# Weight fold and FFN on one core: x transposed in strips 1 to 3 of the fold only, four transpositions at a time

## The chip, the cores and the metric

One core of a Trainium2 chip runs the program. The metric is the device time of one execution in microseconds. TensorE is PE in the profile (PEld its weight loads), VectorE is DVE, ScalarE is ACT, the queue of SyncE that issues every DMA is SP.

## What is computed

```python
# x (8, 512, 2048), itok (8,), weight (2048, 2048), lora_a (8, 16, 2048), lora_b (8, 2048, 16), codes (2048, 2048)
base = jnp.einsum('bsi,oi->bso', x, weight) + bias
low = jnp.einsum('bsi,bri->bsr', x, a_sel)          # a_sel = lora_a[adapter_id]
delta = jnp.einsum('bsr,bor->bso', low, b_sel)
y = base + scale[:, None, None] * delta
w = _dequant_nf4(codes, absmax)
out = x + jnp.einsum('bsd,od->bso', y, w) + bias2
```

All in float32. The kernel multiplies the two weight matrices first (the "fold"), and then x by the folded matrix.

## The kernel before

**Two stages.** The fold makes W = w times weight, in NS = 4 strips of 512 output columns. A strip is 17 jobs (`S1`), 68 in all (`JOBS`); job g is step s = g mod 17 of strip g // 17. In a job PE multiplies one tile of `weight` (in step 0 the columns of lora_b) with the strip's dequantised codes `wq`: 16 k-steps of three matmuls 128x512 (`three`, lines 1035 to 1037; float32 is split into a high and a low half, and the third small product is left out). In the first step of a strip 32 bias matmuls follow (lines 1115 and 1116). The second stage then multiplies x by the folded matrix in 448 products, by a scheme with seven products in place of eight (A11, A12, S2, SS1, S3, S4, A22), whose operands are sums of blocks.

**What else the fold does, job by job.** All engines go through the jobs in one fixed order that is written out by hand.
- DVE: in odd steps from 3 on, and in step 0, the sums of the folded weights (`weight_sums`, 797 to 802), one dequantisation of a 128x512 piece of codes for the next strip in strips 0 to 2 (`dequantise_a` and `_b`, 741 to 773), sums of x (`x_sum`, 808 to 818), the low halves of the next job's tile (`split_lo`, 788, two) and of a transposed piece (`piece_lo`, 782).
- ACT: copies the last job's result out of PSUM (`evacuate`, 563), then the factors for the piece (`make_downs`, 538 and 540), the high halves of the next tile (`split_hi`, 553), the ladders and rungs of the next piece (`make_ladders` 517 and 518, `make_ups` 526 to 533), the high half of a transposed piece (`piece_hi`, 547), and the copies of transposed x (`copy_group`, 571).
- PE: beside the matmuls, four transpositions of a dequantised piece together (`transpose_piece`, 1030, after k-step 9 or 4), and those of x.
- SP: the DMAs, in one queue. It waits in its program order, and what stands behind a waiting DMA waits too. The second half of the tile for job g + 2 is loaded when job g is done; the first half when half of job g is done.

**x in the fold.** x is brought into the scheme's form here: 128 groups of 128x512. A group is loaded into `x_nat` (three buffers), transposed by four PE instructions into `tr_x` (two PSUM banks), copied by ACT into `rq`, which has one 2 KB slot for each of the seven blocks. Four groups are a unit (32 units); DVE makes four sums of a unit, and one DMA of 1792 KB stores all seven blocks to `xc_d` (`store_x_sums`, line 311). The first copy of the next unit waits for that store. `groups_of` places the groups: one in an odd job, three in an even one, in jobs 1 to 64; a transposition stands alone between two k-steps:

```python
for c, i in enumerate(groups):
    if 0 <= k - x_start[c] < QK:
        transpose_x(i, k - x_start[c])
```

The sums of weights go by a DMA of 896 KB (`store_w_sums`, line 316) every second job. In strips 0 and 2 the two stores fall in the same job, in strips 1 and 3 in different ones.

## Time and profile before

| | |
|---|---|
| median of 3 runs | 2314.99 us (2314.47 to 2316.05) |
| the profiled execution, its own time | 2315.77 us |
| its span | 2314.0 us |
| PE busy | 2210.7 us (96%) |
| DVE busy | 1684.9 us (73%) |
| ACT busy | 1115.7 us (48%) |
| DMA, mean | 238 GB/s, 75.8% of 16 engines' span |
| jobs of the fold end between | 161 and 983.5 us |
| four x transpositions, PE, x512 | 271 ns each |

The page gives busy time by engine and by line; a busy PE there is an upper measure, since the spans of pipelined matmuls overlap. Where the fold ends a job, ACT copies the result at once, so the start of line 563 on ACT is the job's end on PE to within 0.05 us. The difference of two such starts is a job's length.

### The profile page before, as it was taken

How to read it: one execution, taken by the hardware profiler on the slowest of the kernel's cores; microseconds unless marked ns; L12 is line 12 of the kernel's file. 1: busy time of each engine (PE TensorE's matmuls, PEld its weight loads, DVE VectorE, ACT ScalarE, POOL GpSimd, SP SyncE). 2: the span in 40 equal slices, each digit the busy share in tenths (PEclk: the TensorE clock that was granted, in tenths of full speed). 3: DMA queues.
4: the chain of work that ended last, by engine and by line, in shares of the span. 5: the costliest groups of instructions: out<-in, count | busy, mean ns of one | idle time of the engine just before them, and what ended most of it. 6: DMA issues, size and time to landing. Idle time of an engine off the chain costs nothing.

```text
span 2314.0 us, 37569 instructions
## 1 busy us (share of the span) xinstructions
PE 2210.7 (96%) x15112; PEld 2012.9 (87%) x15112; DVE 1684.9 (73%) x2400; ACT 1115.7 (48%) x1494; POOL 0.2 (0%) x4
## 2 busy tenths in 40 slices
PE   1389999999999999999999999999999999999999
PEld 1368877887888787899999999999999999999999
DVE  8888886897888434387777776666776666776665
ACT  6666665675666333254444443333444433433332
POOL 0000000000000000000000000000000000000000
PEclk9799999999999999999999999999999999999999
DMA  5248885888687699777777887777887787877775
GB/s 119 69 151 260 256 269 187 267 261 254 221 267 244 207 301 290 248 249 242 236 231 240 262 258 242 241 245 242 277 267 240 241 246 243 297 246 240 240 244 173
DMA packets 399331, 550.51 MB, mean 238 GB/s; under 512 B 41624, under 2 KB 256280, under 8 KB 399032
## 3 DMA queue, kind: packets, MB, share of 16 engines
q1 hardware_dynamic: 399160, 548.12, 75.8%
q8 instruction: 121, 1.98, 0.3%
q14 instruction: 50, 0.41, 0.1%
HBM read 421.66 MB, written 127.42 MB: 237 GB/s over the span
## 4 chain that ended last, share of the span: by engine, by line
PE 56%; DMA 0%; DVE 0%; issue 0%; ACT 0%; DVEq 0%
PE ps L1037 18%; PE ps L1035 18%; PE ps L1036 18%; PE ps L1078 1%; DMA comb_raw<-wc_d 0%; PE ps L1067 0%; ACT comb L584 0%; DVE res L903 0%; DVE res L910 0%; DVE res L888 0%; DVE low_st L848 0%; DVE comb L825 0%; DVEq L908 0%
## 5 line engine op out<-in xcount | busy, mean ns | idle before, releaser
L1035 PE MATMUL ps<-comb,xs 128*128 128x256 f32 (+1 forms) x3584 | 1014.6, 283 | 0.9 <-issue 0.9
L1037 PE MATMUL ps<-comb,xs 128*128 128x256 f32 (+1 forms) x3584 | 1014.7, 283 | 0.0
L1036 PE MATMUL ps<-comb,xs 128*128 128x256 f32 (+1 forms) x3584 | 1009.3, 282 | 0.0
L589 ACT CAST xs<-xr 128x1024 fp32r<-128x1024 f32 x427 | 447.8, 1051 | 638.9 <-DMA xr<-xc_d 638.2
L831 DVE TENSOR_TENSOR xs<-xr,xs 128x1024 fp32r<-128x1024 f32 x427 | 522.5, 1224 | 299.7 <-ACT xs L589 297.4
L1036 PEld LDWEIGHTS ps<-comb,xs 128*128 128x128 f32 x3584 | 677.8, 189 | 5.3
L1035 PEld LDWEIGHTS ps<-comb,xs 128*128 128x128 f32 x3584 | 676.7, 189 | 1.3 <-issue 1.3
L1037 PEld LDWEIGHTS ps<-comb,xs 128*128 128x128 f32 x3584 | 676.7, 189 | 0.0
L1035 PE MATMUL ps<-wq,tile 128*128 128x512 f32 x1088 | 477.4, 439 | 3.4 <-DVE wq L782 3.4
L1037 PE MATMUL ps<-wq,tile 128*128 128x512 f32 x1088 | 428.9, 394 | 0.0
L1036 PE MATMUL ps<-wq,tile 128*128 128x512 f32 x1088 | 427.2, 393 | 0.0
L1035 PEld LDWEIGHTS ps<-wq,tile 128*128 128x128 f32 x1088 | 206.2, 189 | 73.0 <-DVE wq L782 3.8
L1037 PEld LDWEIGHTS ps<-wq,tile 128*128 128x128 f32 x1088 | 205.7, 189 | 45.6
L1036 PEld LDWEIGHTS ps<-wq,tile 128*128 128x128 f32 x1088 | 207.9, 191 | 22.5 <-issue 1.0
L788 DVE TENSOR_TENSOR tile<-raw,tile 128x1024 fp32r<-128x1024 f32 x136 | 161.6, 1220 | 35.2 <-ACT tile L553 35.2
L553 ACT CAST tile<-raw 128x1024 fp32r<-128x1024 f32 x136 | 138.9, 1048 | 48.6 <-DMA raw<-in_L_cond_weight_dram 45.5
L1046 PE MATMUL ps<-ident,x_nat 128*128 128x128 f32 x512 | 139.0, 271 | 0.0
L1030 PE MATMUL ps<-ident,wq_nat 128*128 128x128 f32 x256 | 44.2, 301 | 86.8 <-DVE wq_nat L773 86.8
L1030 PEld LDWEIGHTS ps<-ident,wq_nat 128*128 128x128 f32 x256 | 34.0, 154 | 98.7 <-DVE wq_nat L773 79.5
L563 ACT COPY cs<-ps 128x512 f32<-128x512 f32 x64 | 37.6, 588 | 161.2 <-PE ps L1037 161.2
L571 ACT COPY rq<-ps 128x512 f32<-128x512 f32 x128 | 75.2, 587 | 55.7 <-PE ps L1046 42.6
L910 DVE TENSOR_TENSOR res<-ps,res 128x512 f32<-128x512 f32 x128 | 88.6, 692 | 14.0 <-DVE res L880 0.5
(92 smaller groups left out, 1710.1 us busy)
## 6 DMA issues: line engine op xcount, KB each, us to landing
xr<-xc_d SPq DMA_DIRECT2D x427, 512.0 KB, 4.0
raw<-in_L_cond_weight_dram SPq DMA_DIRECT2D x128, 512.0 KB, 4.5
xc_d<-rq SPq DMA_DIRECT2D x32, 1792.0 KB, 7.5
x_nat<-in_x_dram SPq DMA_DIRECT2D x128, 256.0 KB, 3.8
res<-in_x_dram SPq DMA_DIRECT2D x64, 512.0 KB, 5.5
out_dram<-res SPq DMA_DIRECT2D x128, 256.0 KB, 5.0
wc_d<-cs SPq DMA_DIRECT2D x32, 896.0 KB, 4.6
comb_raw<-wc_d SPq DMA_DIRECT2D x28, 1024.0 KB, 8.3
```

The lines of the kernel that those rows point to most:

```text
L553: nc.scalar.copy(tile[slot][:, HI, :, :], raw[slot][:, LO, :, :]).then_inc(s_hi, 1)
L563: nc.scalar.copy(cs[:, h:h + 5:4, :], acc[g % 2][:, :].rearrange("p (c o) -> p c o", c=2)).then_inc(s_evac, 1)
L571: nc.scalar.copy(rq[:, GROUP_OF[r], :, :], tr_x[i % 2][:, :].rearrange("p (t s) -> p t s", t=QK)).then_inc(s_xcp, 1)
L589: nc.scalar.copy(xs[f][:, HI, :, :], xr[f][:, LO, :, :]).then_inc(s_xhi, 1)
L788: tt(tile[slot][:, LO, :, :], raw[slot][:, LO, :, :], tile[slot][:, HI, :, :].bitcast(F32), ALU.subtract).then_inc(s_lo, 1)
L831: tt(xs[f][:, LO, :, :], xr[f][:, LO, :, :], xs[f][:, HI, :, :].bitcast(F32), ALU.subtract).then_inc(s_xlo, 1)
L910: tt(dst, bank_d[u][:, :], dst, ALU.add).then_inc(s_lev, 1)
L1030: last = nc.tensor.transpose(tr_q[n % 2][:, t * P:(t + 1) * P], wq_nat[n % 2][:, t * P:(t + 1) * P], ident[:, :])
L1035: nc.tensor.matmul(out_ap, t_hi, m_hi, start=first, stop=False)
L1036: nc.tensor.matmul(out_ap, t_hi, m_lo, start=False, stop=False)
L1037: return nc.tensor.matmul(out_ap, t_lo, m_hi, start=False, stop=last)
L1046: ins = nc.tensor.transpose(tr_x[i % 2][:, t * P:(t + 1) * P], x_nat[i % 3][:, t * P:(t + 1) * P], ident[:, :])
```

## The change

- `x_step(i)` puts group i after k-step 3 + 6i counted from the first k-step of job 17. So 128 groups take 48 jobs (17 to 64), and none stands in strip 0. Three jobs (a round, 48 k-steps) hold eight groups, two units: the first job after k-steps 3, 9 and 15, the second after 5 and 11, the third after 1, 7 and 13.
- The four transpositions of a group follow each other.
- `x_nat` has two buffers instead of three; SP loads group i + 2 when group i is transposed. The freed 2 KB hold `a21_t`: the first group of a unit is copied there, not into the slot of S3, so that it need not wait for a store.
- A unit's blocks go to memory by two DMAs: A11 and A12 (512 KB, `store_x_blocks`) once ACT has copied them, the other five (1280 KB, `store_x_sums`) when the sums are made. The second copy of the next unit waits for the store of the five, the third for that of the two.
- The copies, sums, loads and stores are placed by `groups_in` in bands of k-steps. A copy whose transposition stands after k-step 8 to 10 comes behind the ladders on ACT, one after k-step 0 to 3 ahead of `split_hi`, one after 11 or later at the next job's head.

```diff
-    GROUP_OF = [S3, A22, A11, A12]
+    GROUP_OF = [None, A22, A11, A12]
...
+    def x_step(i):
+        return S1 * KT + 6 * i + 3
+
+    def groups_in(g, first, last):
+        return [i for i in range(4 * UNITS) if KT * g + first <= x_step(i) < KT * g + last]
...
-        x_nat = [at(f"x_nat{i}", 176 + 2 * i, [P, QD], F32) for i in range(3)]
+        x_nat = [at(f"x_nat{i}", 176 + 2 * i, [P, QD], F32) for i in range(2)]
+        a21_t = at("a21_t", 180, [P, QK, P], F32)
...
-                if i >= 3:
-                    sp.wait_ge(s_tr, i - 2)
+                if i >= 2:
+                    sp.wait_ge(s_tr, i - 1)
...
                 sp.wait_ge(s_sums, 4 * (m + 1))
-                sp.dma_start(xc_d[p, :, :, c * QK:(c + 1) * QK, :].rearrange("f p k t -> p f k t"),
-                             rq[:, :, :, :]).then_inc(s_xst, 16)
+                sp.dma_start(xc_d[p, S2:, :, c * QK:(c + 1) * QK, :].rearrange("f p k t -> p f k t"),
+                             rq[:, S2:, :, :]).then_inc(s_xst, 16)
+
+            def store_x_blocks(m):
+                p, c = divmod(m, 2)
+                sp.wait_ge(s_xcp, 4 * (m + 1))
+                sp.dma_start(xc_d[p, :S2, :, c * QK:(c + 1) * QK, :].rearrange("f p k t -> p f k t"),
+                             rq[:, :S2, :, :]).then_inc(s_xsa, 16)
...
-                if g % 2 == 0 and len(ahead) > 2:
-                    load_group(ahead[2])
+                n = pieces_of(g)
+                for k in range(KT):
+                    for i in groups_in(g, k - 1, k):
+                        if i + 2 < 4 * UNITS:
+                            load_group(i + 2)
+                    if k == 8 and g + 2 < JOBS:
+                        load_half(g + 2, 0)
+                    for i in groups_in(g, k - 4, k - 3):
+                        if i % 4 == 3:
+                            store_x_blocks(i // 4)
+                    for i in groups_in(g, k - 8, k - 7):
+                        if i % 4 == 3:
+                            store_x_sums(i // 4)
+                    if k == 11 and n is not None and n + 2 < NS * PIECES:
+                        load_codes(n + 2)
...
                 act.wait_ge(s_tr, i + 1)
                 if r == 0 and m:
+                    act.wait_ge(s_sums, 4 * m - 2)
+                if r == 1 and m:
                     act.wait_ge(s_xst, 16 * m)
-                nc.scalar.copy(rq[:, GROUP_OF[r], :, :], tr_x[i % 2][:, :].rearrange("p (t s) -> p t s", t=QK)
+                if r == 2 and m:
+                    act.wait_ge(s_xsa, 16 * m)
+                nc.scalar.copy(rq[:, GROUP_OF[r], :, :] if r else a21_t[:, :, :], tr_x[i % 2][:, :].rearrange("p (t s) -> p t s", t=QK)
...
+                for i in groups_in(g, 8, 11):
+                    copy_group(i)
                 for i in turned_in(g):
                     piece_hi(i)
...
+            def transpose_x(i):
+                pe.wait_ge(s_xn[i % 2], 16 * (i // 2 + 1))
...
+                for t in range(QK):
+                    last = nc.tensor.transpose(tr_x[i % 2][:, t * P:(t + 1) * P], x_nat[i % 2][:, t * P:(t + 1) * P],
+                                               ident[:, :])
```

**SP's queue around job 41** (strip 2, step 7; `wc_d` is the weight sums' store, `xc_d` the x store, `raw` half a tile, `code_t` codes). Before, job 41:

```order
L316 DMA wc_d<-cs 128x7x256
L311 DMA xc_d<-rq 128x7x512
L298 DMA raw_57<-in_L_cond_weight_dram 128x8x128
L282 DMA code_t<-in_L_ffn_codes_dram 128x512
L306 DMA x_nat_69<-in_x_dram 128x512
L298 DMA raw_58<-in_L_cond_weight_dram 128x8x128
```

Now job 41, a first job of a round:

```order
L325 DMA wc_d<-cs 128x7x256
L320 DMA xc_d<-rq 128x2x512
L309 DMA x_nat_67<-in_x_dram 128x512
L314 DMA xc_d<-rq 128x5x512
L301 DMA raw_57<-in_L_cond_weight_dram 128x8x128
L309 DMA x_nat_68<-in_x_dram 128x512
L285 DMA code_t<-in_L_ffn_codes_dram 128x512
L301 DMA raw_58<-in_L_cond_weight_dram 128x8x128
```

Now the end of job 42 and the beginning of job 43, the round's third job:

```order
L314 DMA xc_d<-rq 128x5x512
L301 DMA raw_56<-in_L_cond_weight_dram 128x8x128
L325 DMA wc_d<-cs 128x7x256
L309 DMA x_nat_68<-in_x_dram 128x512
L309 DMA x_nat_67<-in_x_dram 128x512
```

The x store is in two parts with a load of x between them, and in the third job a load of x stands behind the stores and half a tile.

**ACT in job 41.** Before, from the evacuation to the last rung:

```order
L563 COPY cs<-ps 128x2x256
L571 COPY rq<-ps 128x512
L538 ACTIVATE rung_a<-ladder_61 128x512
L540 ACTIVATE rung_b<-ladder_61 128x512
L553 CAST tile_51<-raw_55 128x1024
L553 CAST tile_52<-raw_56 128x1024
L517 ACTIVATE ladder_60<-code_t,consts 128x512
L518 ACTIVATE ladder_60<-code_t,consts 128x512
L547 CAST wq_50<-ps 128x4x128
L526 ACTIVATE wq_nat_62<-ladder_60,consts 128x512
```

Now, from the second half of the tile on:

```order
L564 CAST tile_52<-raw_56 128x1024
L528 ACTIVATE ladder_60<-code_t,consts 128x512
L529 ACTIVATE ladder_60<-code_t,consts 128x512
L586 COPY rq<-ps 128x512
L558 CAST wq_50<-ps 128x4x128
L537 ACTIVATE wq_nat_62<-ladder_60,consts 128x512
```

The copy of a unit's second group (line 586 here) stands inside the job, ahead of the piece's cast and of the rungs for the next piece; before, the copy that waited for the store stood at the next job's head.

## Rows read from the trace of the kernel before

**Rows 1.** Windows; job pairs of strips 2 and 3, one store.
```profile
core 0: us, PE busy (x) PEld busy (x) DVE busy (x) ACT busy (x) POOL busy (x), PEclk, DMA share, GB/s
603.20:627.88 24.68, 24.68 (x122) 19.85 (x121) 22.00 (x34) 16.96 (x26) 0.00 (x0) 1.00 0.84 262
635.00:638.00 3.00, 3.00 (x17) 2.38 (x16) 2.90 (x5) 3.00 (x6) 0.00 (x0) 1.00 1.02 362
807.40:831.20 23.80, 23.80 (x113) 19.04 (x112) 9.01 (x12) 7.32 (x10) 0.00 (x0) 1.00 0.97 304
```

**Rows 2.** Timeline of ACT, one row at a job's end: strips 2, 3, last jobs.
```profile
603.25 0.59 ACT L563 COPY cs<-ps 128x512 f32<-128x512 f32 x1 [1.59 <-PE ps L1037]
...
627.93 0.59 ACT L563 COPY cs<-ps 128x512 f32<-128x512 f32 x1 [1.59 <-PE ps L1037]
...
819.47 0.59 ACT L563 COPY cs<-ps 128x512 f32<-128x512 f32 x1 [6.35 <-PE ps L1037]
...
843.28 0.59 ACT L563 COPY cs<-ps 128x512 f32<-128x512 f32 x1 [4.51 <-PE ps L1037]
...
972.68 0.59 ACT L563 COPY cs<-ps 128x512 f32<-128x512 f32 x1 [6.00 <-PE ps L1037]
...
983.56 0.59 ACT L563 COPY cs<-ps 128x512 f32<-128x512 f32 x1 [8.16 <-PE ps L1037]
```

**Rows 3.** Timeline of ACT and PE where strip 1 begins.
```profile
333.86 0.59 ACT L563 COPY cs<-ps 128x512 f32<-128x512 f32 x1 [1.59 <-PE ps L1037]
...
346.13 0.79 PE L1035 MATMUL ps<-wq,tile 128*128 128x512 f32 x1 [3.45 <-DVE wq L782]
...
351.85 0.40 PE L1115 MATMUL ps<-wq,b_hl 128*2 128x512 f32 x1
```

**Rows 4.** Timeline of PE: two waits in the dequantisation ahead of the fold.
```profile
110.59 0.66 PE L1030 MATMUL ps<-ident,wq_nat 128*128 128x128 f32 x4 [2.62 <-DVE wq_nat L773]
...
111.32 0.39 PE L1036 MATMUL ps<-wq,tile 128*128 128x512 f32 x1
...
132.67 0.66 PE L1030 MATMUL ps<-ident,wq_nat 128*128 128x128 f32 x4 [3.94 <-DVE wq_nat L773]
...
133.81 0.63 PE L1037 MATMUL ps<-wq,tile 128*128 128x512 f32 x1
```

**Rows 5.** Timeline of DVE, one job that stores weight sums (strip 2).
```profile
603.87 0.42 DVE L797 TENSOR_TENSOR cs<-cs 128x256 f32<-128x256 f32 x1 [2.13 <-ACT cs L563]
...
605.35 0.42 DVE L741 TENSOR_SCALAR wq_nat<-wq_nat 128x512 f32<-128x512 f32 x1
...
607.61 0.68 DVE L818 TENSOR_TENSOR rq<-rq 128x512 f32<-128x512 f32 x1
...
612.52 2.35 DVE L788 TENSOR_TENSOR tile<-raw,tile 128x1024 fp32r<-128x1024 f32 x2
```

**Rows 6.** Timeline of ACT, the same job.
```profile
611.06 0.57 ACT L547 CAST wq<-ps 128x512 fp32r<-128x512 f32 x1
611.52 0.72 ACT L526 ACTIVATE wq_nat<-ladder,consts 128x512 f32<-128x512 bf16 x1
...
612.76 0.71 ACT L533 ACTIVATE rung_b<-ladder,consts 128x512 f32<-128x512 bf16 x1
```

**Rows 7.** Timeline of SP and of ACT, the next such job.
```profile
630.13 0.38 SPq L316 DMA_DIRECT2D wc_d<-cs  x1
633.00 0.37 SPq L311 DMA_DIRECT2D xc_d<-rq  x1
633.41 0.66 SPq L298 DMA_DIRECT2D raw<-in_L_cond_weight_dram  x1
...
640.80 0.59 ACT L571 COPY rq<-ps 128x512 f32<-128x512 f32 x1 [0.44 <-DMA xc_d<-rq]
```

**Rows 8.** DMA issues: landings in the whole run; of raw in strip 2.
```profile
xc_d<-rq SPq DMA_DIRECT2D x32, 1792.0 KB, 7.5
...
DMA to landing us min/median/max: 3.9/4.6/9.4
```

More of the change, by code:

```diff
@@ L233, in adaln_ffn_kernel @@
         s_a_st = sem("a_sel_stored")
-        s_xn = [sem(f"x_group_loaded{i}") for i in range(3)]
+        s_xn = [sem(f"x_group_loaded{i}") for i in range(2)]
         s_tr = sem("x_group_transposed")
@@ L397, in _ @@
             load_codes(8)
-            for i in range(3):
+            for i in range(2):
                 load_group(i)
@@ L649, in _ @@
                 j, s = divmod(g, S1)
-                n, groups = pieces_of(g), groups_of(g)
+                n = pieces_of(g)
                 if s != 1 and g:
                     evacuate(g - 1)
-                if groups_of(g - 1):
-                    copy_group(groups_of(g - 1)[-1])
+                for i in groups_in(g - 1, 11, KT):
+                    copy_group(i)
                 if s == 1:
@@ L661, in _ @@
                     make_downs(n)
-                if groups and g % 2 == 0:
-                    copy_group(groups[0])
+                for i in groups_in(g, 0, 4):
+                    copy_group(i)
                 if 0 < g < JOBS - 1:
@@ L666, in _ @@
                     split_hi(g + 1, 1)
-                if groups and g % 2 == 0:
-                    copy_group(groups[1])
+                for i in groups_in(g, 4, 8):
+                    copy_group(i)
                 if n is not None and n + 1 < NS * PIECES:
                     make_ladders(n + 1)
+                for i in groups_in(g, 8, 11):
+                    copy_group(i)
                 for i in turned_in(g):
@@ L804, in x_sum @@
             def x_sum(m, step):
-                a11, a12, s2, s1, a21, s4, a22 = (rq[:, f, :, :] for f in range(NF))
+                a11, a12, s2, s1, s3, s4, a22 = (rq[:, f, :, :] for f in range(NF))
+                a21 = a21_t[:, :, :]
                 if step == 0:
@@ L943, in _ @@
                 j, s = divmod(g, S1)
[L944 to L945 removed]
+                n = pieces_of(g)
                 if s == 1:
@@ L954, in _ @@
                     weight_sums(j - 1, HK - 1)
+                for i in groups_in(g - 1, 11, KT):
+                    x_sums_after(i)
                 if n is not None:
                     dequantise_a(n)
-                if g % 2 and groups_of(g - 1):
-                    x_sum((g - 3) // 2, 3)
-                if n is not None:
                     dequantise_b(n)
-                if g % 2 == 0 and groups:
-                    x_sum(m, 0)
+                for i in groups_in(g, 0, 4):
+                    x_sums_after(i)
                 if 0 < g < JOBS - 1:
@@ L967, in _ @@
                     piece_lo(i)
-                if g % 2 == 0 and groups:
-                    x_sum(m, 1)
-                    x_sum(m, 2)
+                for i in groups_in(g, 4, 11):
+                    x_sums_after(i)
                 if j == NS - 1:
@@ L1082, in multiply_tile @@
                 j, s = divmod(g, S1)
-                groups = groups_of(g)
-                x_start = (0, 5, 10) if g % 2 == 0 else (12,) if g == 1 else (10,)
                 for k in steps:
@@ L1098, in multiply_tile @@
                         last.then_inc(s_wquarter, 1)
-                    for c, i in enumerate(groups):
-                        if 0 <= k - x_start[c] < QK:
-                            transpose_x(i, k - x_start[c])
+                    for i in groups_in(g, k, k + 1):
+                        transpose_x(i)
                     if k == (4 if s == 0 else 9):
```

51 lines of the change are left out of this document (19 added, 32 removed).

## Prediction

> **What bounds the kernel now.** I read the table of windows first, then the ends of jobs, then the waits of each engine job by job. In strip 2 PE is busy for the whole of a pair of jobs (24.68 of 24.68 us), DVE for 22.0, ACT for 17.0, and the DMA engines for 0.84 of it [rows 1]. The ends of jobs repeat to a hundredth: a pair takes 24.68 us in strip 2 [rows 2], as it does in strips 0 and 1, and the waits that the trace gives for PE between 134 and 984 us are one, at the beginning of strip 1 [rows 3]. So the fold goes by what PE has to do, and everything else is hidden, but by little: while the x store moves, the queue carries 362 GB/s at a share of 1.02, and one pair of strip 3 stands at 0.97 [rows 1]. In the second stage PE is full too; the change does not touch it, and I cost it at nothing.
>
> **Transpositions, the gain.** The last jobs hold neither codes nor x: 983.56 - 972.68 = 10.88 us, 0.68 per k-step. A pair of strip 3 holds 16 single transpositions of x: 23.81 - 21.76 = 2.05, or 0.128 us each. A pair of strip 2 holds two blocks of four of a piece besides: 24.68 - 23.81 = 0.87, or 0.435 us a block [rows 2]. Four singles cost 0.512, a block 0.435; 128 groups times 0.077 give **9.9 us less**. Where the groups stand changes nothing in that sum, as long as PE is the bound. Strip 0 gets shorter by its 124 + 4 singles (16.4 us), strips 1 to 3 longer by the rest.
>
> **The boundary of strips 0 and 1, a gain.** Job 17 takes 351.85 - 333.81 = 18.0 us where its work is 10.88 + 0.435 + 0.51 = 11.8. PE waits 3.45 us in it for DVE's line 782, the last piece's low half, and the matmul behind the wait takes 0.79 us: the granted clock has fallen to the lower level, 1.2 GHz [rows 3]. Now DVE has no sum of x in that job ahead of the piece (0.6 us less), and PE has three blocks ahead of k-step 12 and gets there at 12 x 0.68 + 3 x 0.435 = 9.5 us in place of 8.9. It waits from 9.5 to 11.7, 2.2 us. After a wait of 2.62 us the next matmuls took 0.39 us, at 2.4 GHz, after one of 3.94 they took 0.63 [rows 4]; I take it that 2.2 leaves the clock up. The job then ends at 14.9 us with 12.6 of work: 2.3 lost in place of 6.2, **3.9 us less**. Gains in all: 13.8 us.
>
> **The stores, the loss.** Call a job heavy if it stores weight sums. Times in the next lines run from a job's start on PE. A heavy job with the x store behind it: the weight sums are issued at 630.13 - 627.88 = 2.25, the store of 1792 KB at 5.1, and it lands at 640.80 - 627.88 = 12.9 [rows 7]. Alone it needs 7.5 us [rows 8]. The two stores and the tile's half follow each other in the queue, and a half tile issued 0.4 us behind the x store lands after up to 9.4 us in place of 4.6 [rows 7, 8]: what is issued later comes later. So it does not help that the five blocks are issued at 3.5 now (behind a load that waits for the group of k-step 3, 4 x 0.68 + 0.435 = 3.2). Ahead of them stand the same half tile and weight sums, their own two blocks, and in addition a load of x (0.26 MB at 362 GB/s [rows 1], 0.7 us). The five land at **13.6 us** in a heavy first job. Before, the copy that waited for this was at the next job's head and waited 0.44 us [rows 7]. Now the copy of the second group waits for it inside the job, with the cast of a piece and the three rungs of the next piece behind it on ACT.
> - ACT then needs 0.5 for the copy, 0.5 for the cast, and 612.76 - 611.52 + 0.6 = 1.85 for the rungs [rows 6]: done at 16.4. The first job has 10.88 + 4 x 0.435 = 12.6 us, so ACT enters the second 3.8 us late.
> - There evacuation and copy take 1.0 (4.8), DVE's two sums 1.2 (6.0), its dequantisation 612.52 - 605.35 less one sum = 6.6 (12.6), the first half tile 2.35/2 (13.8) [rows 5]. The second job has 12.2 us of work. **PE waits 1.6 us.**
> - In the third job DVE needs 1.15 + 0.6 + 0.6 for what it still owes, so the next five blocks are issued at 2.3. A store's first bytes move 2.4 us after its issue (7.5 less 1.84 MB at 362 GB/s). The queue then carries 3.6 us of blocks, 1.6 of half a tile, 2.6 of weight sums, 0.7 of x: that load lands at 13.3. It is the group of k-step 13, since x_nat has two buffers, and PE wants it at 14 x 0.68 + 3 x 0.435 = 10.8. **PE waits 2.5 us.**
>
> This is 4.1 us for a round whose first and third jobs are heavy. There are four with a dequantisation in all three jobs: from step 3 and 9 of strip 1, from 7 and 13 of strip 2. The three that follow a round with a heavy second job meet ACT late already. In that round's third job the second copy waits until 2.2 + 2.4 + 3.6 = 8.2, and copies, two casts of half tiles, ladders, cast and rungs bring ACT to 14.8 of 12.6 us: 2.2 late, and 2.1 more to wait. So 4.1 + 3 x 6.2 = 22.7 us. Smaller ones: 1.5 us for x at the end of strip 1, 0.2 to 0.4 in five third jobs, 1.2 in sum. Bounds for these stores: nothing, if the five blocks came in time, and 30 us, if every such round paid 6.2 and the small ones doubled.
>
> **Strip 3.** There is no dequantisation to delay, but x loads and stores come 8 groups in 3 jobs in place of 2 a job: 0.96 MB or 2.65 us more in a pair that stands at 0.97 of 23.8 us already where operands of the second stage are loaded too [rows 1]; such a pair asks for 25.7 us of the queue and has 24.1. There are a few such pairs. I take 4 us, between 0 and 10.
>
> Edits with one answer: `a21_t`, the new waits of the first and third copies and the order of DVE's sums cost nothing in themselves, since the first and the third copy wait for things done long before (a sum of the unit before, a store of 512 KB issued ahead of the five). DVE's whole work still fits: 22.0 us in a pair [rows 1] and 1.33 sums of 0.6 more make 22.8 of 24.9.
>
> **Sum.** 2315.8 of the profiled execution - 13.8 + 22.7 + 2.7 + 4 = 2331.4; the median is 0.8 lower than that execution, so I say **2330.6 us**.
>
> **The Trainium skill on the store.** By "DMA: Bandwidth & Descriptors", section "Anatomy of one DMA", a DMA takes about 2.0 us and its bytes at 436 GB/s: 5.0 us for 1.31 MB. By that page alone the five blocks would land at 8.5 us, ahead of ACT's turn, and the sum would be 2302. The trace does not agree: a store alone takes 7.5 where the page gives 6.2. The same page, section "Queues, rings and completion order", says that each DMA engine consumes its ring's descriptors in order; by that rule, which the 9.4 us of the half tile bear out, a store waits for what was issued ahead of it.
>
> **Rivals.**
> - *The whole gain.* The five blocks come before ACT wants them, because they move in gaps of the queue; ACT wants them at about 9.0 (line 547 began at 611.06 - 603.20 = 7.9 [rows 6], and a copy and a sum more stand ahead of it). For it: they are issued 1.6 us earlier than the old store and are 29% smaller. Against it: the queue is full from the weight sums on. 2315.0 - 13.8 = **2301 us**. This one ends on the other side; it decides if the store's landing in a heavy first job is under 10 us. Chance 0.22.
> - *Part of it.* The stores delay ACT, but DVE and the loads catch up: half of my 29.4 us. 2316 us, from 2309 to 2322. Chance 0.23.
> - *The clock falls too.* A wait of 2.5 us at k-step 13, or of 3.7 where ACT was late, may bring what 3.45 us brought: 2.8 us more each, for four of them 11 us. **2342 us**. For it: rows 3; against it: the 2.62 us of rows 4. Chance 0.15.
> - *Blocks of x cost more than blocks of pieces*, so that the change does not do what it says: 9.9 us more, 2340. The two are the same instruction with the same shapes. Chance 0.02.
>
> My forecast has 0.38, from 2322 to 2338. The range from 2303 to 2343 leaves out most of the first rival's lower half and the end of the third. By 0.2%, 4.6 us, which is about what a measurement of this kernel can tell from no change, faster is 0.24, the same 0.13, slower 0.63. The whole gain and the lower end of the second case make the first, the middle of the second case the next.
>
> **What would show it.** Right: on ACT, copies of x inside a job that wait for `xc_d<-rq` three to five us in heavy first jobs; PE waits for DVE's line of the tile's low halves at the beginning of some second or third jobs, and for `x_nat` in third jobs; pairs of strip 0 at 22.6 us; x blocks at 0.43 us; job 17 at 14.9 us. Wrong: no wait of PE in strips 1 and 2, stores that land in 6 us after a heavy beginning, or a second stage that starts later or slower for a reason of its own.

## The result, and the profile after

| | before | changed |
|---|---|---|
| median | 2314.73 us (2313.59 to 2316.05, 4 runs) | 2368.70 us (2364.43 to 2372.28, 4 runs) |
| ratio | | 1.0232 (95%: 1.0213 to 1.0252) |
| profiled execution, its own time | 2315.77 us | 2364.43 us |
| its span | 2314.0 us | 2362.5 us |
| end of the fold (evacuation of job 67) | 983.56 us | 1032.45 us |

Slower by 54 us of the median, or 48.7 between the two profiled executions. The whole of it lies in the fold: the last evacuation comes 48.9 us later, and what follows takes as long as before. The side was forecast, the size was not (2330.6, up to 2343).

The page of the changed kernel, its row of PE's clock and of the DMA engines in 40 slices, and the transfers to memory and to `x_nat`:

```profile
PEclk9699999999999999999999999999999999999999
DMA  5135448888888779887777787777987777987775
...
xc_d<-rq SPq DMA_DIRECT2D x32, 1280.0 KB, 6.9
x_nat<-in_x_dram SPq DMA_DIRECT2D x128, 256.0 KB, 5.1
```

The median store of five blocks lands 6.9 us after its issue, where the store of all seven took 7.5 [rows 8]: 29% fewer bytes, 0.6 us. The queue is fuller than before, so this is not the price of the bytes alone: a load of x needs 5.1 us, where the page of before gave 3.8.

What PE waited for in the fold, waits in sum, number and longest:

```profile
PE ps L1071 <- DMA x_nat<-in_x_dram: 28.8, 15, 5.2
PE ps L1060 <- DVE tile L805: 7.5, 4, 2.4
PE ps L1060 <- DVE wq L799: 2.7, 1, 2.7
```

Before there was one wait there, 3.45 us [rows 3]. Now there are twenty: 28.8 us for x loads that have not landed, 7.5 for the low halves of the next tile, 2.7 in job 17. And ACT, on its copies of x:

```profile
ACT cs L574 <- PE ps L1062: 119.3, 36, 14.6
ACT rq L586 <- DMA xc_d<-rq: 108.2, 28, 10.1
```

108.2 us in 28 copies wait for a store of x, against 12.5 us in 10 copies before.

**The first heavy round**, jobs 20 to 22 of strip 1, as forecast step by step. Job 20 starts at 369.67. From the changed kernel's timeline of ACT (start in us, duration, engine, line, operation, and in brackets what it waited for):

```profile
383.05 0.59 ACT L586 COPY rq<-ps 128x512 f32<-128x512 f32 x1 [4.36 <-DMA xc_d<-rq]
383.54 0.59 ACT L558 CAST wq<-ps 128x512 fp32r<-128x512 f32 x1
...
385.86 0.58 ACT L574 COPY cs<-ps 128x512 f32<-128x512 f32 x1
...
404.49 0.59 ACT L586 COPY rq<-ps 128x512 f32<-128x512 f32 x1 [1.93 <-DMA xc_d<-rq]
...
406.35 1.06 ACT L564 CAST tile<-raw 128x1024 fp32r<-128x1024 f32 x1 [0.33 <-DMA raw<-in_L_cond_weight_dram]
```
SP's queue in the same timeline (start is that of the issue; the second column is not the time to landing):

```profile
398.53 0.38 SPq L314 DMA_DIRECT2D xc_d<-rq  x1
398.95 0.53 SPq L301 DMA_DIRECT2D raw<-in_L_cond_weight_dram  x1
400.00 0.83 SPq L325 DMA_DIRECT2D wc_d<-cs  x1
400.87 4.11 SPq L309 DMA_DIRECT2D x_nat<-in_x_dram  x1
```
And PE's timeline, the start of job 22 and the wait inside it:

```profile
396.31 0.47 PE L1060 MATMUL ps<-wq,tile 128*128 128x512 f32 x1 [1.56 <-DVE tile L805]
...
410.47 0.68 PE L1071 MATMUL ps<-ident,x_nat 128*128 128x128 f32 x4 [2.96 <-DMA x_nat<-in_x_dram]
410.88 0.70 PE L1060 MATMUL ps<-wq,tile 128*128 128x512 f32 x1
411.38 0.63 PE L1061 MATMUL ps<-wq,tile 128*128 128x512 f32 x1
```

The five blocks land at 383.05 - 369.67 = 13.4 us into the job (forecast 13.6), ACT comes to the second job's evacuation at 385.86, 3.7 us late (3.8), PE waits 1.56 us before job 22 (1.6), the next five blocks are issued 398.53 - 396.31 = 2.2 us into that job (2.3), and the x load behind them, half a tile and the weight sums holds PE for 2.96 us (2.5). The row behind the wait shows what I had left to a rival: a matmul takes 0.63 us in place of 0.39. The clock, in four stretches of the changed kernel (PE busy with its count, then the same for PE's weight loads, DVE, ACT and POOL; granted clock, DMA share, GB/s; the first number is the length of the stretch):

```profile
410.00:414.00 4.00, 3.53 (x12) 2.88 (x13) 1.51 (x3) 1.68 (x4) 0.00 (x0) 0.62 0.91 260
480.00:484.00 4.00, 3.00 (x15) 2.56 (x16) 4.00 (x7) 2.42 (x5) 0.00 (x0) 1.00 0.49 153
692.00:696.00 4.00, 4.00 (x16) 3.30 (x15) 3.76 (x10) 0.63 (x1) 0.00 (x0) 0.71 0.72 261
944.00:948.00 4.00, 2.91 (x9) 2.53 (x10) 0.00 (x0) 0.00 (x0) 0.00 (x0) 0.50 1.10 326
```

After 410 it fell to 0.62 of full on average over 4 us (1.2 GHz while the slow matmuls ran), after the wait of 2.11 us at 481 it stayed up. Summed over the fold in steps of 4 us, (1 - granted clock) times 4 gives 13.8 us lost to the lower level, 3.4 before, all of it there in job 17.

**Price of a block.** A pair of jobs of strip 0 now holds 32 k-steps and two blocks of a piece, and no x:

```profile
159.97 0.59 ACT L574 COPY cs<-ps 128x512 f32<-128x512 f32 x1 [1.69 <-PE ps L1062]
...
182.69 0.59 ACT L574 COPY cs<-ps 128x512 f32<-128x512 f32 x1 [1.70 <-PE ps L1062]
```

182.69 - 159.97 = 22.72 us; less 21.76 [rows 2] that is 0.48 us for a block, not 0.435. Some eight of the matmuls that follow a block take 0.230 instead of 0.227 us start to start. Where single transpositions stand beside a block, as before in strip 2, the matmuls between them run at 0.230 anyway, so that block seemed cheaper; this reading fits the two numbers, and no run tests it by itself.

### The profile page after: what moved, and what is told of

Its sections match the earlier page's. It is cut to its first block, busy times and chain, and to the rows that moved or that the text cites. A ratio compares the mean times of both kernels' runs of the same rounds, so it can differ in the third digit from the quotient of the medians.

```text
span 2362.5 us, 37664 instructions
## 1 busy us (share of the span) xinstructions
PE 2228.2 (94%) x15112; PEld 2038.6 (86%) x15112; DVE 1688.1 (71%) x2400; ACT 1111.0 (47%) x1494; POOL 0.2 (0%) x4
## 4 chain that ended last, share of the span: by engine, by line
PE 54%; DVE 0%; DMA 0%; issue 0%; ACT 0%; DVEq 0%
PE ps L1062 18%; PE ps L1060 18%; PE ps L1061 18%; PE ps L1102 1%; DMA comb_raw<-wc_d 0%; DVE comb L853 0%; PE ps L1091 0%; ACT comb L599 0%; DVE res L916 0%; DVE res L938 0%; DVE res L931 0%; DVE low_st L876 0%; DVE res L926 0%; DVE res L929 0%; DVE u_sum L924 0%
## 5 line engine op out<-in xcount | busy, mean ns | idle before, releaser
L1060 PE MATMUL ps<-wq,tile 128*128 128x512 f32 x1088 | 450.8, 414 | 10.1 <-DVE tile L805 7.5
L1062 PE MATMUL ps<-wq,tile 128*128 128x512 f32 x1088 | 433.5, 398 | 0.0
L1061 PE MATMUL ps<-wq,tile 128*128 128x512 f32 x1088 | 432.6, 398 | 0.0
L1060 PEld LDWEIGHTS ps<-wq,tile 128*128 128x128 f32 x1088 | 209.6, 193 | 52.7 <-issue 10.8
L1062 PEld LDWEIGHTS ps<-wq,tile 128*128 128x128 f32 x1088 | 209.1, 192 | 47.2
L1061 PEld LDWEIGHTS ps<-wq,tile 128*128 128x128 f32 x1088 | 209.9, 193 | 40.0 <-issue 1.0
L564 ACT CAST tile<-raw 128x1024 fp32r<-128x1024 f32 x136 | 138.2, 1048 | 14.7 <-DMA raw<-in_L_cond_weight_dram 14.4
L586 ACT COPY rq<-ps 128x512 f32<-128x512 f32 x96 | 56.3, 587 | 121.8 <-DMA xc_d<-rq 108.2
L1071 PEld LDWEIGHTS ps<-ident,x_nat 128*128 128x128 f32 x512 | 62.8, 142 | 51.8 <-DMA x_nat<-in_x_dram 37.9
L549 ACT ACTIVATE rung_a<-ladder 128x512 f32<-128x512 bf16 x64 | 40.5, 632 | 142.0 <-DVE wq_nat L761 141.8
L1071 PE MATMUL ps<-ident,x_nat 128*128 128x128 f32 x512 | 78.9, 277 | 28.9 <-DMA x_nat<-in_x_dram 28.8
```

What stands on the lines that cost most here:

```text
L549: nc.scalar.mul(rung_a[:, :], down, rung(2)).then_inc(s_rung, 1)
L564: nc.scalar.copy(tile[slot][:, HI, :, :], raw[slot][:, LO, :, :]).then_inc(s_hi, 1)
L586: nc.scalar.copy(rq[:, GROUP_OF[r], :, :] if r else a21_t[:, :, :], tr_x[i % 2][:, :].rearrange("p (t s) -> p t s", t=QK)).then_inc(s_xcp, 1)
L1060: nc.tensor.matmul(out_ap, t_hi, m_hi, start=first, stop=False)
L1061: nc.tensor.matmul(out_ap, t_hi, m_lo, start=False, stop=False)
L1062: return nc.tensor.matmul(out_ap, t_lo, m_hi, start=False, stop=last)
```

## The experiments

Times are medians. The kernel before was timed again beside them, at medians of 2315.7 to 2316.4 us, and the ratios are to these; the changed kernel was not, so differences to its 2368.70 carry an error of 1 to 2 us, besides its own spread of 8 us.

### e1_blocks: blocks of four alone

```diff
-                        if 0 <= k - x_start[c] < QK:
-                            transpose_x(i, k - x_start[c])
+                        if k == x_start[c] + QK - 1:
+                            for t in range(QK):
+                                transpose_x(i, t)
```

> The kernel before with one edit: the four transpositions of an x group follow each other, after the k-step where the last of them stood. Groups stay where they were, with three x_nat buffers and one store. My forecast priced a block at 0.435 us against 0.512 for four singles: that gives 2315 - 9.9 = 2305 us. The theory formed since, from job pairs of strip 0 in the changed kernel (22.73 us for 21.76 of matmuls and two blocks, 0.48 each), says that a block that stands apart costs 0.48, that the piece's block cost 0.435 before only because singles stood beside it, and that the edit gives next to nothing: 2311 to 2315 us, with pairs of strip 2 of 24.5 to 24.7 us in place of 24.68.

2313.31 us (2311.52 to 2315.54), ratio 0.9990 (0.9981 to 1.0000). Two ends of jobs, a pair of strip 2:

```profile
600.24 0.59 ACT L563 COPY cs<-ps 128x512 f32<-128x512 f32 x1 [1.57 <-PE ps L1037]
...
624.86 0.59 ACT L563 COPY cs<-ps 128x512 f32<-128x512 f32 x1 [1.31 <-PE ps L1037]
```

24.62 us for a pair in place of 24.68; a pair of strip 3, with four blocks of x and none of a piece, takes 851.98 - 828.29 = 23.69 in place of 23.81 [rows 2], so a block of x costs (23.69 - 21.76) / 4 = 0.48 us too. A block of four saves next to nothing: over 31 pairs about 2 us. That is the first term of the sum, 9.9 us, fallen.

It is the pairs that show this, not the time of the execution. In job 17 of this run PE waited longer than before, and the clock stayed up (the kernel before lost 3.4 us to it there):

```profile
346.03 0.50 PE L1035 MATMUL ps<-wq,tile 128*128 128x512 f32 x1 [3.65 <-DVE wq L782]
```
The stretch behind it, its granted clock 1.00 (third number from the end):

```profile
348.00:352.00 4.00, 4.00 (x20) 2.00 (x19) 2.24 (x4) 0.59 (x1) 0.00 (x0) 1.00 0.48 140
```

### e2_late_copy: the copy behind the rungs

```diff
-                for i in groups_in(g - 1, 11, KT):
+                for i in groups_in(g - 1, 8, KT):
                     copy_group(i)
...
-                for i in groups_in(g, 8, 11):
-                    copy_group(i)
```

and the same for DVE's sums.

> The changed kernel with one edit: the copy and the sums of a group transposed after k-steps 8 to 10 go to the head of the next job on ACT and DVE, behind the rungs of the next piece, no longer ahead of them. Nothing else moves. If the copy that waits for the five blocks inside a heavy first job is what makes the next piece and the tile's low halves late, PE's waits for the low halves (7.5 us in sum, with one fall of the clock of 1.8 us) go, and the stores of the following job are issued earlier, so that the x waits of third jobs shrink from about 3 us to about 1: 2369 - 10 to - 20, 2349 to 2359 us. If only x loads matter, the waits for the low halves may go but the time stays over 2362.

2351.89 us (2348.30 to 2354.76), ratio 1.0155 (1.0138 to 1.0172): 16.8 us less than the changed kernel. The waits for the low halves are gone; those for x stayed nearly whole, and did not shrink to 1 us each as expected. The two profiled executions differ by 12.8 us (2351.65 and 2364.43), of which 7.5 are waits for low halves and 3.4 waits for x; the clock costs as much as in the changed kernel (13.6 us for 13.8). The other 4 of the 16.8 us are the distance of the changed kernel's median from its profiled execution:

```profile
PE ps L1069 <- DMA x_nat<-in_x_dram: 25.4, 13, 4.0
PE ps L1058 <- DVE wq L797: 2.7, 1, 2.7
```

### e3_x_first: weight sums stored behind a load of x

```diff
-                if s % 2 and s >= 3:
-                    store_w_sums(j, (s - 3) // 2)
...
                         if i + 2 < 4 * UNITS:
                             load_group(i + 2)
+                    if k == 2 and s % 2 and s >= 3:
+                        store_w_sums(j, (s - 3) // 2)
```

(and the one of step 0). In heavy first jobs the edit puts the store of the two blocks ahead of the weight sums; in strip 3 the weight sums also come behind the loads for the second stage.

> The changed kernel with one edit: in a heavy job SP issues the weight sums' store behind the x load of k-steps 0 and 1, no longer ahead of it. In heavy third jobs the load of the group of k-step 13 then has no weight sums ahead of it in the queue (2.6 us). If order in the queue is what makes it late, the four waits for x_nat in the heavy third jobs of strips 1 and 2 (2.96, 3.58, 2.15 and 3.71 us) fall under 1 us and with them three falls of the clock: 2369 - 10 to - 16, 2353 to 2359 us. If instead the two buffers are too few in any order, the waits stay within 1 us of what they are and the time over 2364.

2338.42 us (2335.82 to 2341.49), ratio 1.0098 (1.0083 to 1.0113): 30.3 us less, more than expected. The order of two entries in SP's queue was worth more than half of the loss:

```profile
PE ps L1060 <- DVE tile L805: 12.3, 8, 2.7
PE ps L1071 <- DMA x_nat<-in_x_dram: 5.7, 8, 1.0
```

The x waits fell from 28.8 to 5.7 us, none over 1.0; the waits for the low halves rose from 7.5 to 12.3, perhaps because they are no longer hidden in the others. And the clock falls once only, in job 17: 1.7 us in sum in place of 13.8, although PE waits 2.42 and 2.70 us at two other places; in part that is luck. 23.1 - 4.8 us of waits and 12.1 of the clock are 30.4 us. The fold ends 1032.45 - 1003.28 = 29.2 us earlier; the profiled executions differ by 25.9 only, because the second stage takes 3.3 us longer here (see e5_both).

The edit changes two things at once: the weight sums' bytes are no longer ahead of the load, and SP no longer waits for DVE to make them before it issues the load, 400.06 - 396.85 = 3.2 us into job 22 in place of 400.87 - 396.31 = 4.6. The two were not tried apart.

### e4_no_x_loads

```diff
                 if i >= 2:
-                    sp.wait_ge(s_tr, i - 1)
+                    return
...
-                pe.wait_ge(s_xn[i % 2], 16 * (i // 2 + 1))
+                pe.wait_ge(s_xn[i % 2], 16)
```

> The changed kernel without the x loads from the third group on: PE transposes the same two tiles again and again, so xc_d holds blocks of the wrong rows; all other work is there. This leaves out 33 MB of reads and every wait for x_nat. If waits for x_nat (28.8 us, 6 falls of the clock at 1.8 us) are the larger part of the loss, it is 2369 - 40 = 2329 us, down to 2320 where the lighter queue also lets the five blocks land earlier; the waits for the tile's low halves stay in part. If the loss comes from ACT's wait for the five blocks, the time stays over 2345.

2324.08 us (2321.55 to 2325.88), ratio 1.0036 (1.0024 to 1.0048). As expected: 44.6 us of the loss need the x loads. Left are 6.7 us of waits for low halves. In job 20, which starts at 367.2 here, the five blocks land after 12.4 us in place of 13.4, with no load of x ahead of them:

```profile
379.57 0.59 ACT L586 COPY rq<-ps 128x512 f32<-128x512 f32 x1 [3.37 <-DMA xc_d<-rq]
```

### e5_both: e2 and e3 together

> The changed kernel with the edits of e2_late_copy and e3_x_first together. The first took every wait of PE for the tile's low halves away (7.5 us in the changed kernel), the second all but 5.7 us of the waits for x_nat, but kept 12.3 us for the low halves. If the two are separate mechanisms (ACT held by the copy that waits for the five blocks; x loads behind the weight sums in the queue), both go: e3's 2338 - 12.3 = 2326 us, 2320 to 2330, and what is left over the kernel before is the x waits of strip 3 and small ones. If one only hands its delay on to the other, the waits come back in one of the two places and the time is 2335 or more.

2322.93 us (2317.87 to 2324.19), ratio 1.0025 (1.0016 to 1.0035). The two edits add up (16.8 + 30.3 = 47.1 us, and 45.8 came off); the two mechanisms are separate. PE waits 3.3 us for x in all and no more for low halves, although ACT still waits 52.4 us in 21 copies:

```profile
ACT rq L586 <- DMA xc_d<-rq: 52.4, 21, 6.0
...
PE ps L1069 <- DMA x_nat<-in_x_dram: 3.3, 5, 0.9
```

The same placement in strips 1 to 3, the same two buffers and the same two stores lose 6.5 us in place of 54. And most of these 6.5 are not lost in the fold: its last evacuation starts at 984.37, 0.8 us after that of the kernel before. The second stage takes 5.5 us longer (2320.3 - 984.37 = 1335.9 for 2314.0 - 983.56 = 1330.4), where the changed kernel took as long as before. The edit of e3_x_first reaches there. Near the end of strip 3 the weight sums' store now stands behind the loads for the second stage. Its row before, in SP's timeline:

```profile
964.01 0.37 SPq L316 DMA_DIRECT2D wc_d<-cs  x1
```
In this run, SP's, ACT's and PE's rows:

```profile
972.62 0.38 SPq L325 DMA_DIRECT2D wc_d<-cs  x1
...
977.45 0.59 ACT L574 COPY cs<-ps 128x512 f32<-128x512 f32 x1 [9.62 <-DMA wc_d<-cs]
...
998.55 0.33 PE L1089 MATMUL ps<-ident,low_rep 128*128 128x128 f32 x1 [1.21 <-DVE low_rep L905]
```

The wait for `low_rep`, 1.0 to 1.4 us, stands in all six runs with that edit and in none of the other ten; how the late store leads to it was not followed. The clock also falls twice in the second stage of this execution (granted 0.66 from 1007 to 1012 us and 0.84 from 1335 to 1345), 3.4 us in sum, and not once in that of the kernel before. One such fall stands in six runs without the edit too, so it does not belong to the edit alone.

### e8_one_store: two transfers made one again

```diff
-                sp.dma_start(xc_d[p, S2:, :, c * QK:(c + 1) * QK, :].rearrange("f p k t -> p f k t"),
-                             rq[:, S2:, :, :]).then_inc(s_xst, 16)
+                sp.dma_start(xc_d[p, :, :, c * QK:(c + 1) * QK, :].rearrange("f p k t -> p f k t"),
+                             rq[:, :, :, :]).then_inc(s_xst, 16)
```

> The changed kernel with one part undone: one store of all seven blocks (1792 KB) where the five are stored now; the third copy waits for it too. In a heavy first job nothing changes in when the last block lands (the same bytes follow each other in the queue). In a third job the blocks that moved in the second job now stand ahead of half a tile and of x, 1.5 us more: four x waits grow by 1.5 us each and ACT is later: 2369 + 5 to + 15 us. If a second transfer costs the queue something in itself, as a fixed price of a store, the single one is better: 2355 to 2367.

2395.47 us (2391.39 to 2399.32), ratio 1.0345 (1.0329 to 1.0360): 27 us more than the changed kernel: the direction of the queue theory, but about twice the upper end of what it gave.

```profile
PE ps L1067 <- DMA x_nat<-in_x_dram: 51.3, 24, 6.3
PE ps L1056 <- DVE tile L801: 9.2, 5, 2.7
```

The two transfers are a part of the change that helps. That they do so by moving 1.5 us of blocks out of the place where x waits is not shown: there are 24 x waits in place of 15, not four longer ones, the third copy waits for the later store as well (ACT waits 135.7 us for stores of x in place of 108.2), and the clock costs 18.8 us in place of 13.8.

### e7_spread: the groups over jobs 2 to 64

```diff
-        return S1 * KT + 6 * i + 3
+        return 2 * KT + 63 * i // 8 + 3
```

> The changed kernel with one number changed: the groups stand 7.875 k-steps apart from job 2 to job 64, about two a job as in the kernel before, not 6 apart from job 17. Two buffers, two stores, blocks of four and the order in the queues stay. If putting 128 groups in 48 jobs is the cause (a queue that is busy 0.93 of strips 1 and 2 in place of 0.84), PE's waits for x_nat and for the low halves nearly vanish: 2311 to 2320 us. If two buffers or the order of stores and loads are the cause at any density, waits of some 10 us and more stay, now in strip 0 too: over 2330.

2331.92 us (2328.48 to 2333.44), ratio 1.0065 (1.0052 to 1.0079), between the two answers. 37 of the 54 us go with the density, and the x waits with them (1.1 us), but not those for low halves:

```profile
PE ps L1060 <- DVE tile L805: 12.7, 9, 2.4
PE ps L1060 <- DVE wq L799: 5.1, 1, 5.1
```

Neither "density alone" nor "order at any density" holds. The edit also puts the groups after other k-steps of their jobs. The shares in the expectation were too high as well: from 357 to 570 and from 600 to 800 us the DMA engines were busy 0.87 and 0.86 in the changed kernel, and before, from 357 to 560 and from 600 to 800 us, 0.79 and 0.80. What holds ACT here is another thing than in the changed kernel: it waits 83.0 us for halves of tiles in place of 14.4, and 24.5 for stores of x in place of 108.2.

### e11_spread_all and e13_spread_half_first

e11_spread_all is e7_spread with the edits of e5_both and of e6_early_piece (below).

> The spread placement of e7_spread (2331.9 us, 17.8 us of waits of PE, all but 1 of them for low halves) with the edits of e5_both and the early piece. If the waits for low halves in e7_spread come from ACT held by a copy inside a job, as in the changed kernel, they all go, and the wait of 5.1 us in job 17 too: 2332 - 18 - 3 = 2311 us, 2308 to 2314, about what the kernel before gives with the early piece. If two x_nat buffers are too few at this density, x waits come up instead: over 2318.

2334.51 us (2332.68 to 2337.86), ratio 1.0082 (1.0067 to 1.0098). A miss: 17.5 us of waits for low halves remained. ACT is not held by a copy there, but by the second half of the tile. SP's and ACT's rows of one such job (PE's job had ended at about 435.0):

```profile
437.30 0.37 SPq L314 DMA_DIRECT2D xc_d<-rq  x1
...
438.28 1.05 SPq L301 DMA_DIRECT2D raw<-in_L_cond_weight_dram  x1
```
ACT's row, the cast of that half tile:

```profile
447.13 1.05 ACT L564 CAST tile<-raw 128x1024 fp32r<-128x1024 f32 x1 [4.86 <-DMA raw<-in_L_cond_weight_dram]
```

SP waits for DVE's sums of x before it stores them, the half tile stands behind, is issued 3 us late and then moves behind 1280 KB. e13_spread_half_first turns these two round:

```diff
+                for i in groups_in(g, 2, 8):
+                    if i % 4 == 3:
+                        store_x_sums(i // 4)
```

behind `load_half(g + 2, 1)`, in place of the stores from k-step 10 on.

> e11_spread_all (2334.5 us) with one edit on SP: a store of the five blocks that stands behind k-step 10 of a job is issued after the second half of the tile for job g + 2, no longer ahead of it. In e11_spread_all ACT waits 4 to 5 us for that half in six jobs of strip 1, and SP issues it 3.2 us after the job's end because it waits in order for the sums of x. If that order is what is left of the loss, the 17.5 us of waits for low halves go: 2334 - 15 to - 20 = 2314 to 2319 us. If two x_nat buffers or the store's bytes are the cause, x waits of PE take their place and the time stays over 2326.

2323.66 us (2320.34 to 2324.55), ratio 1.0032 (1.0020 to 1.0043): 10.9 us less, short of what was expected. The waits for low halves are 7.1 us now. What remains of them wasn't followed. In the profiled executions (2320.93 us, before 2315.77) the fold ends 1.5 us later than before, at 985.07, and the second stage takes 3.5 us longer.

### e14_round_half_first: the same edit on the placement in rounds

> e9_both_early (2317.8 us) with the same edit on SP. There PE waits for low halves no more, 3.7 us of x waits are left. In the second job of a round the half tile now stands ahead of the five blocks (3.6 us in the queue), so ACT gets it earlier in the third job, but the five land 1.6 us later and hold the copy of that job's first group. If the two cancel: 2315 to 2320 us. If ACT is held longer than the half tile gains, waits for low halves return and it is over 2322.

2319.68 us (2315.33 to 2323.05), ratio 1.0016 (1.0007 to 1.0026), against 2317.82 of e9_both_early: the two cancel, as said there. PE waits 1.8 us for low halves again and 4.2 for x.

### e12_fill: work inside the waits

```diff
+                if i in (15, 31, 71, 87, 100, 116):
+                    g = x_step(i) // KT
+                    pe.wait_ge(s_gsb, g // S1 + 1)
+                    for t in range(8):
+                        nc.tensor.matmul(g_ps[:, :], tile[2 * (g % 2)][:, HI, t, :], wq[g // S1 % 2][:, t, HI, :],
+                                         start=True, stop=True)
```

> The changed kernel with work added on PE: ahead of six groups whose x load comes 2 to 5 us late (jobs 22, 28, 43, 49, 54 and 60) eight matmuls of 128x512 into a free PSUM bank, 1.8 us each time, whose result nobody reads. The time of the waits themselves does not change, since the matmuls stand inside them. If the slow matmuls behind the waits are the clock's fall because PE stood idle, and a shorter idle stretch avoids it, five or six falls at 1.8 us go: 2369 - 9 to - 11 = 2358 to 2360 us. If the clock falls anyway, or the slowness behind a wait has another cause, 2366 to 2371.

2364.89 us (2364.45 to 2366.75), ratio 1.0214 (1.0200 to 1.0228): 3.8 us less, not 9 to 11, and not clear of the noise, since the changed kernel's ratio is 1.0213 to 1.0252. Between the two profiled executions there is no gain at all (2364.45 and 2364.43 us). The wait in job 22 became

```profile
410.66 1.98 PE L1069 MATMUL ps<-wq,tile 128*128 128x512 f32 x8
412.89 0.66 PE L1077 MATMUL ps<-ident,x_nat 128*128 128x128 f32 x4 [0.26 <-DMA x_nat<-in_x_dram]
```

and the clock stayed up there. Over the fold 10.2 us are lost to the lower level in place of 13.8, but the fold ends no earlier (1032.91, changed kernel 1032.45): 10.9 us of matmuls were added, and the waits shrank by some 9 only. And the clock fell at two other waits instead (398 and 439 us), and once more in job 49, behind only 1.9 us of idling (793 us in this run):

```profile
792.00:796.00 4.00, 2.99 (x11) 2.44 (x12) 1.17 (x2) 0.19 (x1) 0.00 (x0) 0.76 0.89 211
```

In the changed kernel it did not fall after 2.11 us, nor at 705 us after 2.15. How long PE waited does not settle alone whether the clock falls. Less idling went with a fall saved in jobs 22, 28 and 54, but this run does not show that it saves time.

### e6_early_piece and e10_blocks_early: the boundary, on the kernel before

ACT casts the last piece of strip 0 ahead of the next tile's halves in job 17, DVE makes its low half between the two parts of the dequantisation:

```diff
+                if g == S1:
+                    piece_hi(turned_in(g)[0])
...
+                if g == S1:
+                    piece_lo(turned_in(g)[0])
```

> The kernel before with one edit: in job 17 the halves of the last piece are made early, the cast on ACT ahead of the next tile's, the low half on DVE between the two parts of the dequantisation. PE waits 3.45 us for that low half at k-step 12 and then runs at 1.2 GHz for 5.7 us, 6.2 us over the job's work. If PE's wait is the whole of that loss, the low half is ready about 6 us into the job, PE does not wait, the clock stays at 2.4 GHz, and the kernel takes 2315 - 5 to - 6 = 2309 to 2310 us. If the time there is hidden behind the bias matmuls (DVE and ACT wait for them anyway), nothing is gained: 2315.

2310.43 us (2308.72 to 2310.72, 7 runs), ratio 0.9973 (0.9962 to 0.9983). Job 17 from its start to the first bias matmul, in this kernel's busy time by stretches:

```profile
334.30:346.10 11.80, 11.80 (x58) 9.50 (x57) 9.77 (x17) 7.90 (x12) 0.00 (x0) 1.00 0.81 270
```
The same job in the kernel before:

```profile
333.80:351.85 18.05, 14.60 (x58) 11.16 (x57) 11.12 (x18) 8.37 (x13) 0.00 (x0) 0.81 0.79 251
```

11.8 us without a wait, against 18.05 us with 3.45 of waiting and a mean clock of 0.81. The fold ends 5.8 us earlier, at 977.76.

> The kernel before with two edits: blocks of four as in e1_blocks (0.04 us less in a pair of jobs in strips 0 to 2, 0.12 in strip 3) and the last piece early as in e6_early_piece. 32 pairs at 0.04 to 0.12 are 2 us: 2310.4 - 2 = 2308.5 us if a block of four is worth that beside a piece's block; if e1_blocks owed its 2.5 us to the clock that stayed up in job 17 only, 2310.4 as e6.

2309.07 us (2307.85 to 2309.94, 6 runs), ratio 0.9970 (0.9959 to 0.9982). This version beats both kernels, the one before by 0.3%; its lead of 1.4 us over e6_early_piece is within their intervals.

### e9_both_early: the best of the changed placement

> The changed kernel with the edits of e5_both (2322.9 us) and the one of e6_early_piece (6.0 us on the kernel before). In e5_both PE still waits 2.7 us in job 17, and the clock falls behind it in some runs. If the two places are independent this gives 2323 - 4 to - 5 = 2318 to 2319 us, still no better than the kernel before. If ACT's longer order in job 17 (a copy of x more) delays the piece again, nothing is gained: 2323.

2317.82 us (2314.70 to 2320.94, 10 runs), ratio 1.0008 (0.9999 to 1.0017), as expected: level with the kernel before, 8.7 us behind the best. In the profiled execution, the slowest of the ten, the fold ends at 982.84, 0.7 us before that of the kernel before; the second stage takes 6.0 us longer, with the wait for `low_rep` and two falls of the clock as in e5_both. To leave the weight sums' store where it was in strip 3 was not tried.

## Why the prediction was right in its side and wrong in its size

Three steps made the size wrong, between the profiled executions: the clock's falls behind the new waits, put at nothing in the sum (13 us), the price of a block (8 us), and strip 3 (6 us). The waits that the stores bring in strips 1 and 2 came as a sum as forecast.

**Transpositions, 9.9 us less: wrong.** The step "a pair of strip 2 holds two blocks besides: 0.435 us a block" took a difference of two mixtures as the price of a block that stands alone. Alone it costs 0.48 (pairs of strip 0 after), and e1_blocks shows 0.06 us less a pair in strip 2 and 0.12 in strip 3. The term was 2 us. The rival "blocks of x cost more than blocks of pieces", to which I gave 0.02, was the wrong question: both cost 0.48, in strip 0 after and in strip 3 of e1_blocks.

**The boundary, 3.9 us less: wrong by half.** PE got to k-step 12 at 9.6 us (forecast 9.5), but DVE's low half let it go on at 331.27 - 319.00 = 12.3, not 11.7. The step "no sum of x in that job ahead of the piece, 0.6 us less" took the sum as work on the path; it had covered a wait for ACT, which stands in its place now. From DVE's timeline of the changed kernel:

```profile
323.95 0.69 DVE L777 SCALAR_TENSOR_TENSOR deq_e<-rung_a,deq_e 128x512 f32<-128x512 f32 x1 [0.46 <-ACT rung_b L551]
```
From PE's, the matmul that waits for the low half of the piece:

```profile
331.27 0.50 PE L1060 MATMUL ps<-wq,tile 128*128 128x512 f32 x1 [2.67 <-DVE wq L799]
```

PE waited 2.67 us, the clock fell behind it, and the job took 17.07 us, not 14.9: 4.5 us over its work of 12.6 where it was 6.2 before, 1.7 us less in place of 3.9. "2.2 leaves the clock up" rested on one wait of 2.62 us [rows 4]; waits of that length go either way.

**The stores in heavy rounds, 22.7 and 2.7 us: right in mechanism, and in sum partly by luck.** The landing, ACT's lag, and both waits of PE came within 0.5 us in the round shown. By idle time, strips 1 and 2 lose 12.4 and 13.5 us, 25.9 in all for 25.4 forecast. But the four heavy rounds lose 4.5, 5.7, 4.6 and 7.0 us, 21.8 for 22.7, the last with a wait of 1.91 us for x in its second job that was not forecast, and the smaller waits sum to 4.1 for 2.7. "Alone it needs 7.5 us" read a median over stores in a busy queue as that of a store alone. The term made from it held all the same: the five blocks of job 22, issued at 398.53, landed 404.49 - 398.53 = 6.0 us later, as 2.4 + 3.6 gives. e2_late_copy shows the ACT part (its waits for low halves are 0), e3_x_first the queue part, e5_both that they are two things: with both the fold ends 0.8 us later than before. That the double buffer is too small a reserve was never tried by itself: there was no place for a third.

**Strip 3, 4 us: too small.** Its x waits are 10.4 us, half of them one wait of 5.24 us at 945 us, in job 60, where operand loads of the second stage (1024 and 512 KB, issued at 934.55 and 935.17) stand in the queue ahead of the load of x (936.65). The bound was 10. With the two falls of the clock behind its waits of 2.17 and 5.24 us (5.1 us, counted in the next term) the strip is well outside it.

**The clock: left out of the sum.** I gave it 0.15 as a rival and 11 us. It is 13.8 - 3.4 = 10.4 us more than before, where my sum had 2.8 less. That is the largest error, 13 us. All that spoke against the rival was the one wait of 2.62 us [rows 4]: of ten waits over 1.9 us in this fold, seven brought a fall.

**The sum by what was measured.** Waits 39.1 - 3.4 = 35.7, clock 10.4, transpositions -2: 44.1 of 48.7 us. The idle time of a wait is counted from the modelled end of the matmul ahead, 0.39 us after its start, where the next would have started after 0.23: twenty waits hide 3.3 us so. 1.3 us stay unexplained, and so does why the median lies another 5 us above this execution: the four runs of the changed kernel span 8 us, those of before 2.5.

**The rivals.** The whole gain (2301) fell at its own test: the landing was 13.4 us, not under 10. Here the time in the queue ahead of it decides: without the x load it was 12.4 (e4_no_x_loads). The Trainium skill, "DMA: Bandwidth & Descriptors", section "Anatomy of one DMA", gives a DMA 2.0 us and its bytes at 436 GB/s; the estimate from it had this landing at 8.5 us. That section gives its fit for a single DMA on GpSimd's path, and here SP issues them behind others. The trace does not agree with the estimate: 13.4 us behind the others, and 6.0 us for the five blocks of job 22, where the fit gives 5.0. The same page of the Trainium skill, section "Queues, rings and completion order", has each DMA engine take the descriptors of a ring in order; by that rule a load waits for the stores issued ahead of it. The trace agrees, 28.8 us of x waits and 5.7 in e3_x_first, with the reserve that this edit also lets SP issue the load earlier. The clock rival was no rival to the forecast but an addition to it; with 2330.6 + 11 it would have been 2342, and the price of blocks brings 2350.

## What to carry to other kernels

- Where transfers leave one queue in order, moving one issue by a few instructions can be worth more than the work that a change removes: here 30 us for one place of the weight sums' store. Write down for each issue what stands ahead of it in the jobs where all stores fall together, and what waits behind the engine that waits for it.
- A price taken as the difference of two mixed stretches holds only for that mixture; measure the edit alone first (one run showed 2 us of gain where 9.9 were forecast).
- When a forecast says that PE will wait 2 to 5 us some ten times, add a fall of the clock to most of them (seven of ten here, 1.7 us each, 3.4 behind the longest); and look for the one existing wait of that kind first: removing it gave 6 us for a few lines.
- After an edit to one stage, look at the length of the next one too: in the six runs with the new order of the weight sums' store, which saved 29 us of the fold, the second stage was 2.5 to 6.0 us longer than before, part of it falls of the clock that some other runs have too.

## What the runs showed of the hardware that was not expected

- The clock after a wait: falls behind idle stretches of 2.96, 3.58, 2.41, 3.71, 2.17 and 5.24 us and 2.67 in job 17, none behind 2.11, 2.15 and 1.91 in the same run. In other runs it fell behind 1.94 us (e12_fill) and stayed up behind 2.44 (e12_fill), 2.42 and 2.70 (e3_x_first) and 3.65 (e1_blocks). A fall costs 1.7 us, and 3.4 behind the longest wait and in the kernel before.
- After a block of transpositions, matmuls of 128x512 run at 0.230 us start to start for some eight of them before they are back at 0.227.
- A store of 1280 KB landed in 6.9 us (median of the changed kernel) where one of 1792 KB took 7.5 (median of the kernel before, in a less busy queue), and in 6.0 us where the queue had run empty (job 22).
